# Row maxima turned by the write to DRAM in two-byte pieces, in place of VectorE's 32 x 32 turn

## The reference

```python
Q1, Q2 = jnp.split(Q, 2, axis=-1)
K1, K2 = jnp.split(K, 2, axis=-1)
A1 = jnp.einsum('bhqd,bhkd->bhqk', Q1, K1) * scaling
A2 = jnp.einsum('bhqd,bhkd->bhqk', Q2, K2) * scaling
attn = jax.nn.softmax(A1, axis=-1) - lamb * jax.nn.softmax(A2, axis=-1)
out = jnp.einsum('bhqk,bhkd->bhqd', attn, V)
```

## Time and profile before

| | us |
|---|---|
| median of three runs | 3319.23 (3314.82 to 3320.06) |
| the profiled execution | 3325.93 |
| its span in the profile | 3324.2 |
| VectorE busy | 2795.0 |
| TensorE busy | 3127.3 |
| ScalarE busy | 2541.0 |
| GpSimd busy | 440.3 |

### The profile page before, as it was taken

One profiled execution on the slowest core, in us unless ns is written; L12 is line 12 of the kernel. 1 busy time (PEld: TensorE's weight loads), 2 busy tenths in 40 slices (PEclk: granted clock), 3 DMA queues, 4 the chain that ended last, 5 costly groups with the idle time before them and its releaser, 6 DMA issues. The chain is left out here.

```text
span 3324.2 us, 84031 instructions
## 1 busy us (share of the span) xinstructions
PE 3127.3 (94%) x29395; PEld 1446.7 (44%) x29396; DVE 2795.0 (84%) x2957; ACT 2541.0 (76%) x4691; POOL 440.3 (13%) x637
## 2 busy tenths in 40 slices
PE   8989999999999999999999999999999867999995
PEld 4423332333333333333333333333333656999994
DVE  3589999999999999999999999999999884433343
ACT  3359998998999899899989998999999532333333
POOL 3000000000000000000000000000000443555544
PEclk9989999999999999999999999999999978999997
DMA  6620101011010101111010101011010661222224
GB/s 168 154 47 9 28 21 28 21 31 28 9 30 21 28 9 28 40 25 28 21 28 12 28 21 28 18 34 28 9 30 21 225 237 26 36 38 35 38 36 121
DMA packets 100989, 151.45 MB, mean 46 GB/s; under 512 B 21808, under 2 KB 66728, under 8 KB 98828
## 3 DMA queue, kind: packets, MB, share of 16 engines
q1 hardware_dynamic: 84684, 127.43, 15.3%
q0 software_dynamic: 15904, 18.66, 3.6%
HBM read 85.74 MB, written 60.30 MB: 44 GB/s over the span
## 5 line engine op out<-in xcount | busy, mean ns | idle before, releaser
L707 DVE TENSOR_REDUCE half_max<-scores 128x2 f32<-128x1024 f32 x2064 | 2351.9, 1212 | 56.2 <-PE scores L613 51.8
L681 ACT ACTIVATE probs<-bank 128x512 f32<-128x512 f32 x4104 | 2227.1, 594 | 158.8 <-PE bank L629 91.1
L661 PE MATMUL bank<-probs,V 128*32 128x256 f32 x16384 | 1323.1, 395 | 66.1 <-ACT probs L681 39.2
L613 PE MATMUL scores<-K,Q 48*128 48x512 f16 x4128 | 814.4, 391 | 12.9 <-DVE half_max L707 8.0
L629 PE MATMUL bank<-Q,K 50*128 50x512 f16 x4104 | 796.7, 382 | 0.3 <-ACT probs L681 0.3
L661 PEld LDWEIGHTS bank<-probs,V 128*32 128x32 f32 x16384 | 323.7, 108 | 628.3 <-issue 542.8
L613 PEld LDWEIGHTS scores<-K,Q 48*128 48x128 f16 x4128 | 198.1, 93 | 891.6 <-DVE half_max L707 705.2
L629 PEld LDWEIGHTS bank<-Q,K 50*128 50x128 f16 x4104 | 375.7, 94 | 112.5 <-ACT probs L681 5.0
L583 POOL TENSOR_SCALAR max_parts<-row_max 128x16 f16<-128x16 f32 x65 | 16.5, 254 | 2119.0 <-DVE row_max L713 2119.0
L1517 ACT ACTIVATE h<-u 128x1024 f32<-128x1024 f32 x71 | 75.0, 1057 | 270.0 <-DVE u L1553 270.0
L1481 PE MATMUL pre<-xgT,w 128*128 128x128 f32 x2272 | 267.2, 276 | 4.3 <-ACT xgT L1511 4.2
(11 more groups left out here) (188 smaller groups left out, 1128.7 us busy)
## 6 DMA issues: line engine op xcount, KB each, us to landing
attended<-att SPq DMA_DIRECT2D x64, 256.0 KB, 2.5
W<-in_L_ffn_w_dram SPq DMA_DIRECT2D x16, 1024.0 KB, 6.9
heads<-attended SPq DMA_DIRECT2D x7, 2048.0 KB, 9.4
Q<-q_parts SPq DMA_DIRECT2D x102, 128.0 KB, 5.6
K<-k_parts SPq DMA_DIRECT2D x102, 128.0 KB, 6.0
q_parts<-parts SPq DMA_DIRECT2D x64, 128.0 KB, 2.4
k_parts<-parts SPq DMA_DIRECT2D x64, 128.0 KB, 2.8
xs<-in_L_attn_x_dram SPq DMA_DIRECT2D x8, 512.0 KB, 4.6
```

Of the source, the lines that this page charges most:

```text
L613: mm = nc.tensor.matmul(scores[:, b, h, :], Q[p][r, c, up, t * P:(t + 1) * P], K[p][r, up, kc * TC:(kc + 1) * TC], start=True, stop=True)
L661: mm = nc.tensor.matmul(banks[att_bank[s // KB]][32 * u:32 * u + 32, q], V[wp][:, wk, u // 2, :], probs[:, 4 * s % RING + u, q], start=(wk ...
L681: nc.scalar.activation(probs[:, i % RING, :], banks[tile_bank[i]][:], ACT.Exp, scale=SCALE).then_inc(exp_done, 1)
L707: nc.vector.tensor_reduce(half_max[lc % 2][:, :, up, t, kc], scores[:, b], AX.X, ALU.max).then_inc(max_done[b], 1)
```

## The change

`max_blocks` and VectorE's turn are gone. SyncE waits for GpSimd's `max_parts` and writes it to `md` with the two axes exchanged on the DRAM side, so that `md` holds the same rows as before. `max_parts` is a single buffer, and GpSimd now waits for the write of the chunk before to have landed, where it waited for the turn before. VectorE's order has no `turn_maxima` in the step after `CUT`, nor ahead of the loop.

```diff
-        max_blocks = [sb(f"max_blocks{i}", [P, 32], F16) for i in range(2)]
...
             def load_max(done, lc):
 
                 p, c = lc // CH % 2, lc % CH
-                sp.wait_ge(max_blocks_ready, done)
-                sp.dma_start(md[lc % 2].rearrange("i (b q) -> b i q", q=32), max_blocks[lc % 2][:]
-                             ).then_inc(max_rows_written, 16)
+                sp.wait_ge(max_parts_ready, done)
+                with nc.allow_non_contiguous_dma("maxima turned to rows on their way"):
+                    sp.dma_start(md[lc % 2].rearrange("i q -> q i"), max_parts[:].rearrange("p s i -> p (s i)")
+                                 ).then_inc(max_rows_written, 16)
                 sp.wait_ge(max_rows_written, 16 * done)
...
                 pool.wait_ge(row_max_ready, done)
                 if not first:
-                    pool.wait_ge(max_blocks_ready, done - 1)
+                    pool.wait_ge(max_rows_written, 16 * (done - 1))
...
-            def turn_maxima(done, lc, loaded):
-                dve.wait_ge(max_parts_ready, done)
-                dve.wait_ge(max_loaded[lc % 2], loaded + 1)
-                dve.sem_inc(gate_dve, 1)
-                nc.vector.transpose(max_blocks[lc % 2][:], max_parts[:].rearrange("p s i -> p (s i)")
-                                    ).then_inc(max_blocks_ready, 1)
-
             take_maxima(KB, 0)
             for i in range(PRE, AHEAD):
-                between = None
-                if i == PRE:
-                    between = lambda: turn_maxima(1, 0, 0)
-                maxima(i, i // KB, i % KB, between)
+                maxima(i, i // KB, i % KB)
...
-                        if kb == CUT + 1:
-                            between = lambda: turn_maxima(it * RC + lc + 2, lc + 1, MXD * (it * CH + (lc + 1) // 2))
                         maxima(item, ahead // KB, ahead % KB, between)
```

More of the change, by code:

```diff
@@ L455, in stage_attend @@
         max_parts = sb("max_parts", [P, 2, 16], F16)
-        max_blocks = [sb(f"max_blocks{i}", [P, 32], F16) for i in range(2)]
         scores = ps("scores", [P, 2, 2, TC], F32)
         banks = [ps(f"bank{i}", [P, TC], F32) for i in range(4)]
-        names = ("row_max_ready", "high_ready", "max_parts_ready", "max_blocks_ready", "max_rows_written",
+        names = ("row_max_ready", "high_ready", "max_parts_ready", "max_rows_written",
                  "scoresT_ready", "exp_done", "pv_done", "att_copied", "v_copied")
-        (row_max_ready, high_ready, max_parts_ready, max_blocks_ready, max_rows_written,
+        (row_max_ready, high_ready, max_parts_ready, max_rows_written,
          scoresT_ready, exp_done, pv_done, att_copied, v_copied) = (sem(n) for n in names)
```

## The result

The changed kernel takes 4010.18 us (median of 4 runs, 3995.11 to 4016.88) against 3317.97 us of before: ratio 1.208, 95% interval 1.206 to 1.210. That is 692 us slower, where 6 us faster was forecast and 3520 us was the end of the range.

The account below looks back on a forecast made before the run. VectorE was taken to bound each attention chunk; removing 65 turns at 0.09 us saves 6 us, with the write hidden, so 3319.23 us becomes 3313.2. The range was 3308 to 3520 us.

Parts of the forecast that it names:

- What bounds the chunk: Attention stage: VectorE sets the pace of each 36.60 us chunk; TensorE's own loop comes second at 36.27 us.
- the 6 us of the turn: VectorE in the attention stage: removing 65 turns gains 0.09 us each, 6 us in all.
- Rival D: VectorE's gain is not passed on, as TensorE's stop for the bank takes back 0.1 us; 3319 us, chance 0.06.
- The earlier issue (1.3 us): SyncE's write of the maxima starts when GpSimd is done, 1.29 us earlier than before.
- 4112 packets: Write of the maxima to DRAM: 4096 pieces of 2 B, 257 packets on each of 16 engines.
- part 4: Write of the maxima: 8.5 ns a piece, 3.9 us in all; break-even at 7.7 us, 24 ns a piece.
- Rival B: Small DRAM writes sharing 64 B are dearer, so TensorE waits for the rows; 3394 to 3690 us, chance 0.27.
- dearer end, 47.7 ns a piece: Write of the maxima at the price of 1 KB pieces: 13.9 us, 6.1 us late, 3690 us in all.
- Rival C: Pieces of the write made one after the other for all engines: write 10.4 us, total 3471 us, chance 0.15.
- The price of lateness: TensorE's wait for the rows: 64 chunks each last 36.27 us plus the lateness, in place of 36.60.
- The 1.7: Loads of the maxima into Q: taken as landed 1.7 us after their issue.
- spare time: Between the loaded rows' landing and TensorE's asking for them, in the kernel before: 4.5 us.

Follow-up runs that it names:

- the rows in time: Changed kernel with VectorE's score reductions 30 steps ahead in place of 24: 3490.58 us, ratio 1.050; the kernel before with the same steps: 3349.64 us, ratio 1.010.

## Why the prediction was wrong

- **What bounds the chunk, and the 6 us of the turn:** right. 36.51 us a chunk was measured without the turn, 36.50 was forecast; 8 us (5 to 11) against 6. Rival D is out.
- **The earlier issue (1.3 us) and the 4112 packets:** right. The issue comes 1.38 us after `row_max`. The engines' pace was right for the first 1.5 us only: 9.8 ns a piece and engine, where I took 8.5. (The 0.28 us of the earlier trace rows are 32 slices of 8.75 ns, from the first packet to the last, and not 28; the 8.5 stands.)
- **The step that failed is part 4, the write's length:** 1.16 + 2.2 + 0.5 = 3.9 us. Two of the terms were carried over from the 64 B pieces. Measured over the 65 writes they are 0.94 (issue to first packet) + 7.87 (the packets) + 6.14 (last packet to SyncE) = 14.95 us. The row from which I took the price shows how fast an engine lets go of a piece, and not how fast the target takes it; its 132 packets were never held back. Even an eighth of the pieces lasts 14.7 us, and pieces in 64 B of their own 9.2 to 9.7, over the 7.7 that the write was allowed.
- **Rival B** had the mechanism, at 0.27: small writes are dearer where they share their bytes with others. Its formula was wrong in form: the time does not grow as 257 x (piece - 24 ns) with the number of pieces; for turned pieces of 2 B it goes with how many fall into the same 32 B, by the estimate above some 0.9 us each. Its dearer end, 47.7 ns a piece, gave 13.9 us, near the 14.95 for another reason. The rule of the Trainium skill that speaks for it (DMA: Bandwidth & Descriptors, Specifications: under 512 B read-modify-write) has the right sign, but not the size: in these rows 4096 pieces of 64 B and of 32 B both last 4.5 us, the price starts below 32 B, and the measurement decides. With the same page's rule (the Trainium skill, Rules for kernel authors) that a last dimension that isn't contiguous is one descriptor per element, the trace agrees: 4096 pieces.
- **Rival C** (pieces made one after the other for all engines) is out: 4096 pieces of 64 B last 4.5 us, where C gave 10.4 for 4096 of any size.
- **The price of lateness** was too low even so. With 15.0 us for the write the forecast's own formula gives 64 x (7.3 - 0.33) = 446 us, 3765. Two terms are missing. The loads land 2.8 us after their issue and not 1.7: 70 us. The 1.7 fits the kernel before, where their last packet ends 1.3 us after the issue (1.2 to 1.6); in the changed kernel, behind the long write, it ends at 2.4 (1.6 to 3.1), and TensorE goes on 0.4 later. So the spare time of before was 4.5 us as forecast, and the long write slows the loads too. And TensorE's clock falls at each stop, 2.8 us a chunk: 178 us. Together 694, for 692 measured. The trace has the same in two parts: from `row_max` to the first matmul behind the wait 19.09 us in the mean in place of 11.08, and from there to the next `row_max` 29.03 in place of 26.25, 10.8 us a chunk.
- **The range** ended at 3520 because I cut B in the middle by its chance. Its dear end, 3690, without the clock, would still have been too low.
- Not in the forecast at all: the backed-up pieces hold up other transfers. At 24 steps ahead it shows as the 1.1 us of the loads; with the rows in time the long write still costs some 140 us.

## What to carry to other kernels

A write's cost has two ends: the pace at which engines send packets, which a short transfer shows, and the time until the target has them, which shows in the gap between the last packet and the semaphore. Before a transfer is cut into pieces smaller than any in the trace, ask how many pieces fall into the same few bytes, and price it from the far end. What is issued behind such a write, in the same queue, must be priced with it. A stop of TensorE is to be priced with the slower clock behind it. A turn that a rearranged write can't do cheaply may be had from the DMA's own transpose.

## What the runs showed of the hardware

- Writes to DRAM of 2, 4, 8, 16, 32, 64 B, 4096 each and side by side: 15.6, 15.8, 11.4, 10.4, 4.5, 4.5 us.
- Pieces of 2 B, turned: 512 last as long (14.7 us) as 4096 (15.1); 1024 at pitches of 2, 8, 16, 32, 64 B last 14.4, 4.8, 3.1, 2.8, 2.6 us; in order at pitches of 4, 8, 16, 64 B 4096 last 30, 18.7, 15.4, 9.2 us. Splitting the transfer over two, four or eight makes it 20.5 us and more.
- Of 4096 small writes some 2460 start in the first 1.5 us, then the pace falls from 1600 to some 430 a microsecond. The semaphore comes 3.1 to 8.3 us after the last packet.
- Two loads of 4 KB behind 4096 small writes in the same queue: last data packet 8.2 us after the issue in place of 1.4, and 5.3 us more until TensorE goes on.
- 1024 pieces of 2 B from DRAM into one partition's row last 15.0 us; 4096 into 128 partitions 4.9, into 32 partitions 7.0.
- The DMA's transpose of 128 x 128 two-byte elements from SBUF to SBUF takes 2.3 us from issue to landing.
- A filler of 48 rows of two-byte floats on one half of the array did not keep TensorE at 2.4 GHz (clock 0.864 over the execution), one of 128 rows of four-byte floats nearly did (0.964).
